# The hidden bias product moved from the prologue into the tile loop, and three chunks of the last two matrices' product split in a new order

## The chip, the cores and the metric

One Trainium2 chip, one of its cores. The metric is the device time in microseconds of one execution. TensorE multiplies into PSUM (8 banks of 128 x 512 float32), VectorE, ScalarE and GpSimd work element by element, and SyncE, ScalarE and GpSimd issue the loads and stores.

## The reference

Eight batches of 512 rows of 512 numbers (`x`) go through two layers, both added to `x`:

```python
# layer 1: windowed attention; h = layernorm(x), enc = ctx_1024 (8 x 512 x 512)
score = einsum('nqh,hk,nlk->nql', h, W_a, enc)      # only a window of +-16 rows around p_t counts
align = softmax(masked score) * gauss
x = x + tanh(concat([align @ enc, h]) @ W_c.T)

# layer 2: 64 slots, on xn = layernorm(x); S = slot_init for all batches
slot_mean = S.mean(axis=1)                          # the same row for all tokens
h = gelu(concat([xn, slot_mean]) @ w1 + b1)
alpha = softmax over the top 8 of (h @ w2 + b2) / (|tau| + 0.1)
si = (alpha^T xn) / sum(alpha)
gi = si @ Wih.T + bih;  gh = S @ Whh.T + bhh        # GRU gates; gh does not depend on x
S_new = (1 - z) * n + z * S
y = layernorm(S_new + self-attention(S_new)) * ln_g + ln_b
x = x + (alpha @ (y @ wvp + bvp)) @ wo + bo
```

What the change touches are constants: `Wp = wvp @ wo`, one 512 x 512 product made once; the constant part of the first layer of layer 2, `slot_mean @ w1[512:] + b1`, one bias per hidden unit (`hb`); and `gh = S @ Whh.T`.

## The kernel before, in words

The 4096 rows are 32 tiles of 128 rows (`NT`), four to a batch. A prologue prepares constants, a loop of 32 tile steps does layer 1 for tile s and, some steps later, the first part of layer 2 for the same tiles, and a tail runs the slots' update and the outputs. Each engine has its own hand-written instruction order; semaphores (`S("...")`) tie them together. An engine that waits holds everything behind it in its own order.

Float32 products are mostly done as split products (`mm3`, L455): each factor is a high part (rounded to fp32r) plus a low part (the rest), and three products hi*hi, lo*hi, hi*lo are added in PSUM (lines L456 to L458). A plain `pe.matmul` on F32 tiles is a full-precision product; the profile lists each of these as two instructions.

**Prologue.** On TensorE: warm-up products (L1550); `Wp` in banks 4 to 7 from `WvpT` and `Wo`, in four chunks k of 128 rows, chunks 0 and 1 in full precision (L1575), chunks 2 and 3 split (`SPLIT_WP`); ahead of chunk 3 the 12 transposes of the gathered windows (`turn_windows`, L1559), which wait for the indirect load `encw`; then 16 instructions of the hidden bias product `w1b` x `slotmean` into bank 3 (L1585); then the window product of WaT and the windows (L1617, 16 split blocks over four chunks k and four banks c), one row product (L1624), the window values (L1630), and the loop. Block c of chunk 0 of the window product waits for window part c, and c = 3 for `hb`, because bank 3 holds the bias until VectorE has added `b1` to it (L819).

On VectorE: window positions and masks (L754 to L791, among them four operations on 128 x 288, L775 to L778), the row sums of half of WaT (L782, after its load), the mean of the slots (L793, L794), a load of the flag into a register, the low parts of windows and of WaT (`windows`, `low_key_weights`), `hb`, the low parts of Wc1T (L841), and so on. On ScalarE: the Gaussian, the high parts for `SPLIT_WP` (L1252), the other sums of WaT, then, once all sums are there, WaT's high parts (L1262) and those of windows 1 and 2 (L1265). On GpSimd: the indirect loads (L579) and the low parts for `SPLIT_WP` (L637, L639), counted on `wcs`. On SyncE's queue: `win`, `WvpT`, `WaT`; a wait for the last chunks of `WvpT` and `Wo`; `w1b`; a wait for the gathered windows; `Wc2_raw`, `Wc1T`, four tiles of `xT` and `x`, `w1_raw`, `WhhT`.

**Tile step s** on TensorE (L1809): `score(s)` (12 instructions, waits for the low part of tile s and for the tanh of tile s - 2, which frees its bank), `turn_weights(s - 1)`, `right_half(s)`, at s = 1 `bias_row`, `context(s - 1)`, the first layer and logits of layer 2 where they are due, `extras(s)`, and `turn_rows(s - 2)`, which waits for ScalarE's normalised tile. `extras` holds the products `S @ Whh.T`: the r and z gates at step `GATES_STEP` = 1 into bank `SI` (L1641), the n gate one step later into `H1` (L1648), and two sets of transposes at steps 4 and 6. VectorE's step (L1028) goes: low part of tile s - 3, `scores_max(s)`, statistics of tile s + 3, `weights_of(s)` (the two operations on `stack`, L981 and L982, for which `turn_weights(s)` waits), `extras(s)`, `stats2(s - 1)`. Its `extras(0)` makes seven small constants, `extras(1)` splits `w1` (L929, L930), `extras(2)` adds a row (L933), steps 3 and 4 copy the gates out. GpSimd's step: `residual(s - 1)` (L604, waits for the tanh of that tile), `low_x(s + 2)` (L599), scales.

## Time and profile before

| | us |
|---|---|
| three runs | 348.90, 349.93, 349.70; median 349.7 |
| the profiled execution | 349.35, its span 347.4, mean granted clock of TensorE 0.993 |
| busy over the span | TensorE 329.5 (95%), VectorE 261.0 (75%), ScalarE 198.8 (57%), GpSimd 209.2 (60%) |
| chain that ended last | TensorE 56%, VectorE 14%, GpSimd 7%, ScalarE 7%, DMA 6% |

The span runs from the first to the last instruction; all times of rows are counted from its start. Two things are to be read here: which engine has no idle time in which stretch (busy time by stretch), and, where several engines hand over to each other, the timeline of each: when an operation starts, how long it lasts, and what is said in brackets of the idle time before it. An operation that lasts longer than others of its shape has been held inside.

### The profile page before, as it was taken

The page shows a single profiled execution, that of the slowest core. Times are in us where ns is not written, and L with a number is a line of the kernel's source. Part 1 is how long each engine was busy: PE and PEld are TensorE (multiplying, and loading weights), DVE is VectorE, ACT ScalarE, POOL GpSimd, SP SyncE. Part 2 cuts the span into 40 slices and gives each one's busy share as a digit, 9 for nine tenths or more (in the row PEclk, how much of TensorE's full clock was granted, in tenths as well). Part 3 has the DMA queues.
Part 4 walks back from the last instruction along what each step waited for, and adds up shares of the span by engine and source line. Part 5 has one row for each costly group of instructions (what it writes and reads, how often), then busy time and mean ns, then how long its engine had stood idle before and what let it go on. Part 6 is the DMA issues. An engine that isn't in the chain of part 4 may idle for free.

```text
span 347.4 us, 7118 instructions
## 1 busy us (share of the span) xinstructions
PE 329.5 (95%) x2320; PEld 284.3 (82%) x2320; DVE 261.0 (75%) x749; ACT 198.8 (57%) x406; POOL 209.2 (60%) x353
## 2 busy tenths in 40 slices
PE   8899998999998999999999999999999999999981
PEld 6597856999898998898989989986889886877750
DVE  5989898675789798788787877766953766477873
ACT  3367225567768759668569677666754336313521
POOL 5600156879687776974976884746575335235782
PEclk9999999999999999999999999999999999999997
DMA  7999975232323232232241200008900000000797
GB/s 271 261 321 353 343 216 182 93 114 69 109 74 114 71 98 88 62 119 65 62 122 62 86 9 2 0 0 271 314 1 2 1 2 0 0 0 3 291 393 283
DMA packets 40934, 42.79 MB, mean 123 GB/s; under 512 B 3245, under 2 KB 32045, under 8 KB 40898
## 3 DMA queue, kind: packets, MB, share of 16 engines
q1 hardware_dynamic: 38944, 40.19, 35.4%
q10 hardware_dynamic: 1666, 1.49, 1.3%
q0 software_dynamic: 288, 0.66, 0.7%
q8 instruction: 19, 0.31, 0.4%
q14 instruction: 17, 0.14, 0.1%
HBM read 32.18 MB, written 8.39 MB: 117 GB/s over the span
## 4 chain that ended last, share of the span: by engine, by line
PE 56%; DVE 14%; POOL 7%; issue 7%; ACT 7%; DMA 6%; SPq 1%; DVEq 0%; ACTq 0%; POOLq 0%
PE psum L456 13%; PE psum L457 12%; PE psum L458 12%; PE psum L1741 4%; PE psum L2003 3%; DMA xT<-in_xT 3%; POOL X L604 3%; PE psum L1770 3%; DMA encw<-in_enc,rowi 2%; ACT th L1320 2%; DVE st L971 2%; PE psum L1721 2%; PE psum L1805 1%; DVE xhT_lo L958 1%; PE psum L1952 1%
## 5 line engine op out<-in xcount | busy, mean ns | idle before, releaser
L456 PE MATMUL psum<-GW_hi,hT_hi 128*128 128x292 f32 (+1 forms) x256 | 78.6, 307 | 0.0
L458 PE MATMUL psum<-GW_lo,hT_hi 128*128 128x292 f32 (+1 forms) x256 | 74.0, 289 | 0.0
L457 PE MATMUL psum<-GW_hi,hT_lo 128*128 128x292 f32 (+1 forms) x256 | 73.9, 289 | 0.0
L604 POOL TENSOR_TENSOR X<-X,th 128x512 f32<-128x512 f32 x32 | 38.3, 1196 | 29.0 <-ACT th L1320 28.5
L456 PEld LDWEIGHTS psum<-GW_hi,hT_hi 128*128 128x128 f32 x256 | 48.5, 189 | 1.8 <-issue 1.4
L457 PEld LDWEIGHTS psum<-GW_hi,hT_lo 128*128 128x128 f32 x256 | 48.4, 189 | 0.0
L458 PEld LDWEIGHTS psum<-GW_lo,hT_hi 128*128 128x128 f32 x256 | 48.1, 188 | 0.0
L599 POOL TENSOR_TENSOR hT_lo<-xT,hT_hi 128x512 fp32r<-128x512 f32 x30 | 39.1, 1304 | 2.0 <-DVE stack L982 2.0
L971 DVE BATCH_NORM_STATS2 st<-X 128x6 f32<-128x512 f32 x32 | 22.2, 693 | 22.6 <-POOL X L604 22.6
L456 PE MATMUL psum<-xhT_hi,w_hi 128*128 128x256 f32 x128 | 38.0, 297 | 1.1 <-issue 1.0
L457 PE MATMUL psum<-xhT_hi,w_lo 128*128 128x256 f32 x128 | 36.1, 282 | 0.0
L458 PE MATMUL psum<-xhT_lo,w_hi 128*128 128x256 f32 x128 | 36.1, 282 | 0.0
L1301 ACT ACTIVATE e<-scm,nmr,rr 128x36 f32<-128x36 f32 x32 | 13.3, 417 | 28.8 <-DVE nmr L967 28.7
L456 PEld LDWEIGHTS psum<-xhT_hi,w_hi 128*128 128x128 f32 x128 | 24.3, 190 | 3.9 <-issue 3.8
L1307 ACT CAST aTs<-psum 108x128 fp32r<-108x128 f32 x32 | 8.6, 268 | 30.9 <-PE psum L1795 30.9
L1315 ACT ACTIVATE xh<-X,nm,r2all 128x512 f32<-128x512 f32 x31 | 25.0, 806 | 1.9 <-POOL nm L613 1.9
L457 PEld LDWEIGHTS psum<-xhT_hi,w_lo 128*128 128x128 f32 x128 | 24.4, 190 | 0.0
L458 PEld LDWEIGHTS psum<-xhT_lo,w_hi 128*128 128x128 f32 x128 | 24.3, 190 | 0.0
L456 PE MATMUL psum<-siT_hi,W_hi 128*128 128x256 f32 (+1 forms) x72 | 23.5, 326 | 0.0
L457 PE MATMUL psum<-siT_hi,W_lo 128*128 128x256 f32 (+1 forms) x72 | 23.1, 321 | 0.0
L458 PE MATMUL psum<-siT_lo,W_hi 128*128 128x256 f32 (+1 forms) x72 | 22.9, 318 | 0.0
L958 DVE TENSOR_TENSOR xhT_lo<-psum,xhT_hi 128x512 fp32r<-128x512 f32 x32 | 21.3, 666 | 1.5 <-ACT xhT_hi L1296 1.5
(316 smaller groups left out, 919.0 us busy)
## 6 DMA issues: line engine op xcount, KB each, us to landing
xT<-in_xT SPq DMA_DIRECT2D x32, 256.0 KB, 2.8
X<-in_x SPq DMA_DIRECT2D x32, 256.0 KB, 3.5
out<-ost SPq DMA_DIRECT2D x32, 256.0 KB, 2.8
WhhT<-in_WhhT SPq DMA_DIRECT2D x1, 3072.0 KB, 12.9
WihT<-in_WihT SPq DMA_DIRECT2D x4, 768.0 KB, 6.8
Wo<-in_wo ACTq DMA_DIRECT2D x4, 256.0 KB, 4.4
WvpT<-in_WvpT SPq DMA_DIRECT2D x4, 256.0 KB, 5.2
WaT<-in_WaT SPq DMA_DIRECT2D x1, 1024.0 KB, 12.1
```

The lines of the kernel that those rows point to most:

```text
L456: pe.matmul(out, w_hi, m_hi, start=start, stop=False)
L457: pe.matmul(out, w_lo, m_hi, start=False, stop=False)
L458: return pe.matmul(out, w_hi, m_lo, start=False, stop=stop)
L599: pool.tensor_tensor(hT_lo[:, t % 2, :, :], xT[:, t % 4, :, :], hT_hi[:, t % 2, :, :].bitcast(F32), ALU.subtract).then_inc(S("hl"), 1)
L604: pool.tensor_tensor(tile_x(r), tile_x(r), halves(th[:, :]), ALU.add).then_inc(S("x2"), 1)
L958: v.tensor_tensor(xhT_lo[:, :, dst], bank.rearrange("p (c n) -> p c n", c=KC), xhT_hi[:, :, dst].bitcast(F32), ALU.subtract).then_inc(S("x ...
L971: link(v.bn_stats(st2[:, :], tile_x(r)), "stat")
L1301: act.activation(e[:, :], scm[:, :], ACT.Exp, bias=nmr[:, :], scale=rr1[:, s % 4:s % 4 + 1], accum_out=esum[:, :]).then_inc(S("ex"), 1)
L1315: act.activation(halves((th if r == NT - 1 else xh)[:, :]), tile_x(r), ACT.Identity, bias=nm2[:, :], scale=r2all[:, r:r + 1]).then_inc(S(" ...
L1741: last = pe.matmul(SI[h * NS:(h + 1) * NS, 0:XW], al, X[:, TPB * b + q, h, :], start=q == 0, stop=q == TPB - 1)
L1770: last = pe.transpose(bank[:, c * P:(c + 1) * P], rows_of[:, c * P:(c + 1) * P], ident[:, :])
L2003: last = pe.matmul(out_banks(m)[par], w[at_b, :], mv[g][at_b, :], start=n == 0, stop=n == 2)
```

## The change

- **Hidden bias.** Its 16 products leave the prologue and come, as `hidden_bias`, into tile step 1 (`HIDDEN_STEP`), after `bias_row` and ahead of `context(0)`, into bank `SI` instead of bank 3. The mean of the slots on VectorE moves from the prologue to the end of its `extras(0)`, `hb` to the start of its `extras(2)`. The window product no longer waits for `hb`; ScalarE's gelu waits for it.
- **Gates.** `GATES_STEP` goes from 1 to 2, so the WhhT products and all that follows them (transposes, copies) come one tile step later, and the first of them waits for `hb`, which frees `SI`.
- **Wp.** Chunks 1, 2 and 3 are split instead of 2 and 3. Within a chunk the order is hi*hi for all four banks, then lo*hi, then hi*lo, each waiting for its own low part; the window transposes stand after chunk 3's hi*hi. The low parts are made by VectorE (`low_of_Wp`), two operations a chunk, among its mask operations and ahead of the WaT sums, instead of by GpSimd.
- **VectorE's order.** The WaT sums come last before the flag is loaded; before, they stood after the mask operations L775 to L778.
- **Loads.** SyncE waits for WaT alone, then loads `Wc2_raw`, `Wc1T`, the tiles, `w1_raw`, `w1b`, `WhhT`: `w1b` moves from ahead of `Wc2_raw` to behind `w1_raw`, and the wait for the gathered windows goes.
- Semaphore counts and the places in SBUF follow.

```diff
@@ -34,16 +34,16 @@
-HB_DONE, G_DONE, WM_DONE, EW_DONE = 1, 1, KC + 2, KC + 2
-
-
-HI_WA, HI_ENC, HI_WC1, HI_G, HI_GW, HI_EW = 4, 4 + KC, 6 + KC, 6 + 2 * KC, 6 + 3 * KC, 6 + 4 * KC
-BVZ_DONE, LOW_WP = 5, 5
-
-
-SUMS_DONE, MEAN_DONE, CHUNKS_DONE, LOW_WC1 = 2, 3, 4, 4
-
-SPLIT_WP = (2, 3)
+G_DONE, WM_DONE, EW_DONE, HB_DONE = 0, KC + 1, KC + 1, KC + 2 + NG
+
+
+HI_WA, HI_ENC, HI_WC1, HI_G, HI_GW, HI_EW = 6, 6 + KC, 8 + KC, 8 + 2 * KC, 8 + 3 * KC, 8 + 4 * KC
+BVZ_DONE, LOW_WP = 1, 1
+
+
+SUMS_DONE, CHUNKS_DONE, LOW_WC1, MEAN_DONE = 2, 3, 3, 4 + KC
+
+SPLIT_WP = (1, 2, 3)
 ENC_BANKS = 3
@@ -59,7 +59,7 @@
 SLOT_STEP = [TPB * b + 12 for b in range(NB)]
-BIAS_STEP, GATES_STEP = 1, 1
+BIAS_STEP, HIDDEN_STEP, GATES_STEP = 1, 1, 2
 WARM = 9
...
@@ -488,15 +491,14 @@
         sp.dma_start(WaT[:, :, :], chunks("WaT")).then_inc(S("in_wa"), 16)
-        sp.wait_ge(S(f"in_wo{KC - 1}"), 32)
-        sp.dma_start(w1b[:, :, :], chunks("w1", KC)).then_inc(S("in_w1b"), 16)
-        sp.wait_ge(S("encw"), 16 * NG)
+        sp.wait_ge(S("in_wa"), 16)
         sp.dma_start(Wc2_raw[:, :, :], chunks("WcT", KC)).then_inc(S("in_wc2"), 16)
         sp.dma_start(Wc1T[:, :, :], chunks("WcT")).then_inc(S("in_wc1"), 16)
         for t in range(4):
             xT_load(t)
             x_load(t)
         sp.dma_start(w1_raw[:, :, :], chunks("w1")).then_inc(S("in_w1"), 16)
+        sp.dma_start(w1b[:, :, :], chunks("w1", KC)).then_inc(S("in_w1b"), 16)
         sp.dma_start(WhhT[:, :, :], chunks("WhhT")).then_inc(S("in_whh"), 16)
         sp.wait_ge(S("flag"), 1)
@@ -632,11 +634,6 @@
             if s % 2 == 0 and live(s + 2):
                 scales1(s + 2)
-        for n, k in enumerate(SPLIT_WP):
-            pool.wait_ge(S("wa"), 2 * n + 1)
-            pool.tensor_tensor(Wvp_lo[:, n, :], WvpT[:, k, :], Wvp_hi[:, n, :].bitcast(F32), ALU.subtract).then_inc(S("wcs"), 1)
-            pool.wait_ge(S("wa"), 2 * n + 2)
-            pool.tensor_tensor(Wo_lo[:, n, :], Wo[:, k, :], Wo_hi[:, n, :].bitcast(F32), ALU.subtract).then_inc(S("wcs"), 1)
         pool.wait_ge(S("in_misc"), 16 * 4)
         pool.tensor_copy(bvz[:, :, 0:1], bvp.unsqueeze(2)).then_inc(S("wcs"), 1)
         pool.wait_ge(S("g_lo"), KC)
@@ -771,15 +768,23 @@
         link(v.tensor_copy(rsf[:, :], rsi[:, :]), "win")
         link(v.scalar_tensor_tensor(rend[:, :], pall, REACH, lenf[:, :], ALU.add, ALU.min), "win")
         link(v.tensor_scalar(rend[:, :], rend[:, :], float(T - 1), None, ALU.min), "win")
+
+        def low_of_Wp(k):
+            n = SPLIT_WP.index(k)
+            Wvp_hi, Wvp_lo, Wo_hi, Wo_lo = of_Wp[k]
+            v.wait_ge(S("wa"), 2 * n + 1)
+            v.tensor_tensor(Wvp_lo[:, :], WvpT[:, k, :], Wvp_hi[:, :].bitcast(F32), ALU.subtract).then_inc(S("wplo"), 1)
+            v.wait_ge(S("wa"), 2 * n + 2)
+            v.tensor_tensor(Wo_lo[:, :], Wo[:, k, :], Wo_hi[:, :].bitcast(F32), ALU.subtract).then_inc(S("wplo"), 1)
+
+        low_of_Wp(1)
         r3 = lambda a: a.rearrange("p (b j) -> p b j", b=NB)
         link(v.tensor_tensor(r3(ridx[:, :]), bc(rsf[:, :], WS, 2), bc(jrow[:, :], NB, 1), ALU.add), "win")
         link(v.tensor_tensor(r3(vlo[:, :]), r3(ridx[:, :]), bc(rast[:, :], WS, 2), ALU.is_ge), "win")
         link(v.tensor_tensor(r3(madd[:, :]), r3(ridx[:, :]), bc(rend[:, :], WS, 2), ALU.is_le), "win")
         link(v.tensor_tensor(vlo[:, :], vlo[:, :], madd[:, :], ALU.mult), "win")
-        v.wait_ge(S("in_wa"), 16)
-        for c in range(2, KC):
-            v.tensor_reduce(wsum[:, c:c + 1], WaT[:, c, :], AX.X, ALU.add).then_inc(S("v_prep"), 1)
+        low_of_Wp(2)
         link(v.tensor_reduce(anyv[:, :], r3(vlo[:, :])[:, :, 0:WIN], AX.X, ALU.max), "win")
         link(v.tensor_scalar(madd[:, :], vlo[:, :], 1.0, MASKED, ALU.subtract, ALU.mult), "win")
         link(v.memset(r3(madd[:, :])[:, :, UNI:WS], -MASKED), "win")
@@ -789,9 +794,10 @@
         v.tensor_scalar(flag[:, :], flagf[:, :], -1.0, float(NB), ALU.mult, ALU.add).then_inc(S("flag"), 1)
         v.wait_ge(S("gauss"), 2)
         v.tensor_scalar(gw[0:WP, :], gw[0:WP, :], geo[:, 1:2], None, ALU.max).then_inc(S("first_row"), 1)
-        v.wait_ge(S("in_misc"), 16 * 4)
-        link(v.tensor_reduce(slotmean[:, :], slotT[:, :, :], AX.X, ALU.add), "rt")
-        v.tensor_scalar(slotmean[:, :], slotmean[:, :], 1.0 / NS, None, ALU.mult).then_inc(S("v_prep"), 1)
+        low_of_Wp(3)
+        v.wait_ge(S("in_wa"), 16)
+        for c in range(2, KC):
+            v.tensor_reduce(wsum[:, c:c + 1], WaT[:, c, :], AX.X, ALU.add).then_inc(S("v_prep"), 1)
         v.wait_ge(S("flag"), 1)
         f = v.value_load(flag[0:1, 0:1], min_val=0, max_val=NB)
@@ -815,8 +821,6 @@
         for j in range(1, ENC_BANKS):
             windows(j)
         low_key_weights(1)
-        v.wait_ge(S("pre"), HB_DONE)
-        v.tensor_tensor(hb[:, :], banks[3][:, 0:HC], b1, ALU.add).then_inc(S("first_row"), 1)
         for k in range(2, KC):
             low_key_weights(k)
         with v.If(f > 0):
@@ -917,6 +921,7 @@
         def extras(s):
             if s == 0:
+                v.wait_ge(S("in_misc"), 16 * 4)
                 link(v.scalar_tensor_tensor(itau[:, :], tau, -1.0, tau, ALU.mult, ALU.max), "rt")
                 link(v.tensor_scalar(itau[:, :], itau[:, :], 0.1, None, ALU.add), "rt")
                 link(v.reciprocal(itau[:, :], itau[:, :]), "rt")
@@ -924,6 +929,12 @@
                 link(v.tensor_scalar(b2s[:, :], b2, itau[:, :], None, ALU.mult), "rt")
                 link(v.tensor_tensor(brz[:, 0:2 * KC], bih[:, 0:2 * KC], bhh[:, 0:2 * KC], ALU.add), "rt")
                 link(v.tensor_copy(brz[:, 2 * KC:], bhh[:, 2 * KC:]), "rt")
+            if s == HIDDEN_STEP - 1:
+                link(v.tensor_reduce(slotmean[:, :], slotT[:, :, :], AX.X, ALU.add), "rt")
+                v.tensor_scalar(slotmean[:, :], slotmean[:, :], 1.0 / NS, None, ALU.mult).then_inc(S("v_prep"), 1)
+            if s == HIDDEN_STEP + 1:
+                v.wait_ge(S("pre"), HB_DONE)
+                v.tensor_tensor(hb[:, :], SI[:, 0:HC], b1, ALU.add).then_inc(S("first_row"), 1)
             if s == 1:
                 v.wait_ge(S("in_w1"), 16)
                 link(v.tensor_copy(w1_hi[:, :, :], w1_raw[:, :, :]), "w1s")
@@ -1247,10 +1258,11 @@
         link(act.activation(gall[:, :], gall[:, :], ACT.Exp, scale=-1.0 / DEV))
         act.mul(gall[:, :], gall[:, :], 1.0 / T).then_inc(S("gauss"), 1)
-        for n, k in enumerate(SPLIT_WP):
+        for k in SPLIT_WP:
             act.wait_ge(S(f"in_wo{k}"), 32)
-            act.copy(Wvp_hi[:, n, :], WvpT[:, k, :]).then_inc(S("wa"), 1)
-            act.copy(Wo_hi[:, n, :], Wo[:, k, :]).then_inc(S("wa"), 1)
+            Wvp_hi, Wvp_lo, Wo_hi, Wo_lo = of_Wp[k]
+            act.copy(Wvp_hi[:, :], WvpT[:, k, :]).then_inc(S("wa"), 1)
+            act.copy(Wo_hi[:, :], Wo[:, k, :]).then_inc(S("wa"), 1)
         act.wait_ge(S("in_wa"), 16)
@@ -1321,6 +1333,7 @@
         def gelu(b, h):
             act.wait_ge(S("w1"), 4 * b + 2 * h + 2)
+            act.wait_ge(S("first_row"), 2)
             wait(act, S("lg"), 2 * b - 1)
             for o in range(HC):
                 act.activation(h1T[:, o, h * HT:(h + 1) * HT], HB[h][:, o * HT:(o + 1) * HT], ACT.Gelu,
@@ -1561,30 +1574,22 @@
                     last.then_inc(S("encT"), 1)
-        for k in range(KC):
-            pe.wait_ge(S(f"in_wo{k}"), 32)
-            if k in SPLIT_WP:
-                n = SPLIT_WP.index(k)
-                pe.wait_ge(S("wcs"), 2 * n + 2)
-            for c in range(KC):
-                at_c = slice(c * P, (c + 1) * P)
-                if k in SPLIT_WP:
-                    last = mm3(pe, banks[4 + c], Wvp_hi[:, n, at_c], Wvp_lo[:, n, at_c], Wo_hi[:, n, :], Wo_lo[:, n, :],
-                               False, k == KC - 1)
-                else:
-                    last = pe.matmul(banks[4 + c], WvpT[:, k, at_c], Wo[:, k, :], start=k == 0, stop=False)
-                if k == KC - 1:
-                    last.then_inc(S("wp_mm"), 1)
-            if k == KC - 2:
-                turn_windows()
-
-        pe.wait_ge(S("in_w1b"), 16)
-        pe.wait_ge(S("v_prep"), MEAN_DONE)
-        for o in range(HC):
-            for k in range(KC):
-                last = pe.matmul(banks[3][:, o:o + 1], w1b[:, k, o * P:(o + 1) * P], slotmean[:, k:k + 1],
-                                 start=k == 0, stop=k == KC - 1)
-        last.then_inc(S("pre"), 1)
+        for c in range(KC):
+            pe.wait_ge(S("in_wo0"), 32)
+            pe.matmul(banks[4 + c], WvpT[:, 0, c * P:(c + 1) * P], Wo[:, 0, :], start=True, stop=False)
+        for k in SPLIT_WP:
+            n = SPLIT_WP.index(k)
+            Wvp_hi, Wvp_lo, Wo_hi, Wo_lo = of_Wp[k]
+            for part, (w, m) in enumerate(((Wvp_hi, Wo_hi), (Wvp_lo, Wo_hi), (Wvp_hi, Wo_lo))):
+
+                pe.wait_ge(S("wa"), 2 * n + 2)
+                wait(pe, S("wplo"), 2 * n + part if part else 0)
+                for c in range(KC):
+                    last = pe.matmul(banks[4 + c], w[:, c * P:(c + 1) * P], m[:, :], start=False, stop=k == KC - 1 and part == 2)
+                    if k == KC - 1 and part == 2:
+                        last.then_inc(S("wp_mm"), 1)
+                if k == KC - 1 and part == 0:
+                    turn_windows()
         pe.wait_ge(S("gauss"), 2)
         pe.wait_ge(S("flag"), 1)
@@ -1611,8 +1616,6 @@
                     if c < ENC_BANKS:
                         pe.wait_ge(S("encWT"), max(LOW_WA[0], ENC_DONE[c]))
-                    else:
-                        pe.wait_ge(S("first_row"), 2)
                 at_c = slice(c * P, (c + 1) * P)
                 last = mm3(pe, banks[c][:, 0:NB * WS], WaT_hi[:, k, at_c], WaT_lo[:, k, at_c],
                            encWT_hi[:, k, 0:NB * WS], encWT_lo[:, k, 0:NB * WS], k == 0, k == KC - 1)
@@ -1636,6 +1639,7 @@
             if s == GATES_STEP:
                 pe.wait_ge(S("in_whh"), 16)
+                pe.wait_ge(S("first_row"), 2)
                 for k in range(KC):
                     for h in range(2):
                         last = pe.matmul(SI[h * NS:(h + 1) * NS, :], slotT[:, k, :], WhhT[:, k, h * D:(h + 1) * D],
@@ -1659,6 +1663,16 @@
                 for c in range(KC // 2):
                     last = pe.transpose(SI[:, c * P:(c + 1) * P], ghs[:, KC + c, :], ident[:, :])
                 last.then_inc(S("own"), 1)
+
+        def hidden_bias():
+
+            pe.wait_ge(S("in_w1b"), 16)
+            pe.wait_ge(S("v_prep"), MEAN_DONE)
+            for o in range(HC):
+                for k in range(KC):
+                    last = pe.matmul(SI[:, o:o + 1], w1b[:, k, o * P:(o + 1) * P], slotmean[:, k:k + 1],
+                                     start=k == 0, stop=k == KC - 1)
+            last.then_inc(S("pre"), 1)
         def bias_row():
@@ -1815,6 +1829,8 @@
                 right_half(s)
             if s == BIAS_STEP:
                 bias_row()
+            if s == HIDDEN_STEP:
+                hidden_bias()
             if live(s) and s:
                 context(s - 1)
             if s in TOPK_STEP:
```

## Rows read from the trace of the kernel before

**Rows 1.** Windows view, tile loop: stretch, its length, busy us (x instructions) of each engine.
```profile
61.40:245.00 183.60, 180.04 (x1445) 167.37 (x1446) 143.07 (x499) 129.15 (x271) 133.36 (x262) 1.00 0.27 82
```

**Rows 2.** Timeline, TensorE, prologue: start us, us, engine, line, operation, tiles, count.
```profile
4.93 7.13 PE L1575 MATMUL psum<-Wo,WvpT 128*128 128x512 f32 x16
...
17.31 0.48 PE L456 MATMUL psum<-Wo_hi,Wvp_hi 128*128 128x512 f32 x1
...
20.15 1.84 PE L1585 MATMUL psum<-slotmean,w1b 128*128 128x1 f32 x16
21.85 0.38 PE L456 MATMUL psum<-encWT_hi,WaT_hi 128*128 128x288 f32 x1
...
37.56 0.30 PE L456 MATMUL psum<-GW_hi,hT_hi 128*128 128x292 f32 x1
```

**Rows 3.** Timeline, VectorE, prologue; brackets: idle before it and who released it.
```profile
8.11 0.46 DVE L776 TENSOR_TENSOR vlo<-ridx,rast 128x288 f32<-128x288 f32 x1
8.60 5.68 DVE L777 TENSOR_TENSOR madd<-ridx,rend 128x288 f32<-128x288 f32 x1
...
15.25 1.28 DVE L782 TENSOR_REDUCE wsum<-WaT 128x1 f32<-128x512 f32 x2 [0.47 <-DMA WaT<-in_WaT]
...
18.00 0.41 DVE L793 TENSOR_REDUCE slotmean<-slotT 128x4 f32<-128x256 f32 x1
...
19.36 0.61 DVE L802 CAST encWT_hi<-psum 128x432 fp32r<-128x432 f32 x1 [0.75 <-issue]
...
21.19 1.11 DVE L805 TENSOR_TENSOR encWT_lo<-psum,encWT_hi 128x432 fp32r<-128x432 f32 x2
...
26.33 2.49 DVE L841 TENSOR_TENSOR Wc1T_lo<-Wc1T,Wc1T_hi 128x512 fp32r<-128x512 f32 x4
```

**Rows 4.** Timeline, ScalarE, prologue.
```profile
7.87 0.62 ACT L1252 CAST Wvp_hi<-WvpT 128x512 fp32r<-128x512 f32 x1 [0.88 <-DMA WvpT<-in_WvpT]
...
16.91 2.56 ACT L1262 ACTIVATE WaT_hi<-WaT,wneg 128x512 fp32r<-128x512 f32 x4
19.38 0.91 ACT L1265 CAST encWT_hi<-psum 128x432 fp32r<-128x432 f32 x2
```

**Rows 5.** Timeline, SyncE's DMA queue, first load after its second wait.
```profile
16.12 0.37 SPq L494 DMA_DIRECT2D Wc_raw<-in_WcT  x1
```

**Rows 6.** Timeline, TensorE, end of tile step 1 to score(4).
```profile
45.52 0.50 PE L1805 MATMUL psum<-EW,aTs 108*128 108x256 f32 x2
45.95 3.65 PE L1641 MATMUL psum<-WhhT,slotT 128*64 128x512 f32 x16
49.54 0.40 PE L456 MATMUL psum<-GW_hi,hT_hi 128*128 128x292 f32 x1
...
53.09 1.95 PE L1648 MATMUL psum<-WhhT,slotT 128*64 128x256 f32 x16
...
60.74 0.66 PE L1770 MATMUL psum<-ident,xh 128*128 128x128 f32 x4 [0.98 <-ACT xh L1315]
61.36 0.37 PE L456 MATMUL psum<-GW_hi,hT_hi 128*128 128x292 f32 x1
```

**Rows 7.** Timeline, VectorE, tile steps 0 to 2.
```profile
45.88 0.18 DVE L926 COPY brz<-vecs 128x4 f32<-128x4 f32 x1
...
47.91 1.29 DVE L981 TENSOR_SCALAR stack<-e,ev 128x72 fp32r<-128x72 f32 x1
49.23 1.19 DVE L982 SCALAR_TENSOR_TENSOR stack<-e,ev,stack 128x36 f32<-128x36 f32 x1
...
51.06 1.23 DVE L930 TENSOR_TENSOR w_lo<-w_raw,w_hi 128x1024 fp32r<-128x1024 f32 x1
...
55.40 0.68 DVE L933 TENSOR_TENSOR rows<-psum,rows 128x512 f32<-128x512 f32 x1
```

**Rows 8.** Timeline, GpSimd, tile step 1.
```profile
47.95 1.19 POOL L604 TENSOR_TENSOR X<-X,th 128x512 f32<-128x512 f32 x1 [1.92 <-ACT th L1320]
49.10 1.27 POOL L599 TENSOR_TENSOR hT_lo<-xT,hT_hi 128x512 fp32r<-128x512 f32 x1
```

5 lines of the change are left out of this document (4 added, 1 removed).

## The prediction

> **What bounds the kernel now.** I read the busy time by stretch first. From 61.4 to 245 us TensorE is busy 180.0 of 183.6 us [rows 1]: in the tile loop there is nothing left for it to wait for, so a step that starts late there ends late by the same amount, and work given to TensorE is paid in full unless it falls into a hole. The question is therefore by how much score(4), the product that opens tile step 4 at 61.36 [rows 6], comes earlier or later; from there on the same products stand in the same order but for two sets of transposes that move by one step each (steps 4 and 6 lose what steps 5 and 7 gain), a sum of zero. The timeline of TensorE in the prologue [rows 2] shows an unbroken line from 17.31 to 37.56. The other engines' timelines there [rows 3, 4] show why it can't start the window product much earlier: VectorE first has to sum WaT, turn the windows and make low parts, and ScalarE's rounding hangs on these sums. In steps 1 and 2 [rows 6] the 3.59 us of WhhT products (45.95 to 49.54) stand exactly where VectorE is busy with something that TensorE will need [rows 7]: they are cover, not only work.
>
> I keep the clock of the kernel before (the "old clock") and first shift all by what the prologue wins.
>
> **Part 1, the prologue up to the window product.** Removed from TensorE: the bias product, 1.70 us (20.15 to 21.85 [rows 2]), and the full-precision product of chunk 1. A full-precision chunk costs 3.56 us (7.13 for two), a split one 2.84 (17.31 to 20.15), so 0.7 less. TensorE would be ready some 2.5 us or more ahead of 21.85. But it then waits. VectorE's new line: it is free for the first low part at about 7.6 (one mask operation, 0.49, ahead of the row at 8.11 [rows 3]), when ScalarE, idle for 0.88 us ahead of 7.87 [rows 4], can have made the first high part. Six low parts at 0.62 (2.49 for four of that shape [rows 3]) are 3.7; four mask operations at 0.49 are 2.0, the 5.68 us of L777 being a stretched one; the small operations between the sums and 18.00 are 1.5. That is 14.8. The two sums take 1.28 and give 16.1 if WaT has landed by 14.8, and 16.5 if it lands as before at 15.2. So the sums end where they ended before (16.5), and ScalarE's four WaT roundings (2.47) and two window roundings (0.91 [rows 4]) start 0 to 0.4 us earlier and end at about 19.9 to 20.3. VectorE's 0.75 of loading the flag and 1.83 for window part 0 and WaT part 0 (19.36 to 21.19 [rows 3]) are done by 18.7 to 19.1, but windows 1 and 2 (0.55 each) wait for ScalarE, and the third of 16 blocks of the product starts at 20.5 to 20.9, as if the first had at 19.7 to 20.1. Gain: 21.85 less that, 1.75 to 2.15; I take **1.9**. VectorE's later line (three adds, the low parts of Wc1T) runs without a hole and moves by the same, and the loads come earlier, because SyncE now waits for WaT instead of the gathered windows (16.12 [rows 5]) and w1b is no longer among the first. Bounds: 0.9, if VectorE comes 1 us later to the sums than reckoned (GpSimd is still writing the gather's descriptors when the first low parts run, and no row shows the two together); 2.6 to 2.8, with 2.6 taken, if the two window waits cost nothing (21.85 less 19.1). The low parts that leave GpSimd cost nothing there; nothing of it is waited for until the tile loop.
>
> **Part 2, the tile loop's first steps, old clock.** VectorE gets the mean of the slots after the last operation of its step 0 (ends 46.06 [rows 7]), two operations that took 0.61 (18.00 to the 0.75 us ahead of 19.36 [rows 3]): ready at 46.7. TensorE gets there at 45.52 [rows 6], waits 1.2 us, loads weights (0.2), runs 1.70 and starts context(0) at 48.6; the tanh of tile 0, which must free a PSUM bank for score(2), follows its end: 48.6 + 0.5 + 0.7 (an estimate from the context's 0.50 and a 0.6 to 0.8 us ScalarE pass) is 49.85. score(2) started at 49.54 before; now 49.85, with the WhhT products still to do. w1b is covered: it stands ahead of WhhT in the queue, and WhhT was there at 45.95 without a wait.
>
> Score, turning, right half and context of step 2 take 3.55 (49.54 to 53.09), so TensorE is at the moved WhhT product at 53.4. There it now waits for hb, an addition of 0.15 us on VectorE, because the bank in which the hidden bias lies is the one these products write. Behind that wait stand, on TensorE, the WhhT products, the turning of tile 0 and score(3); nobody else is held by it. When is hb there? Before, VectorE reached that place (its step 2 extras) at 55.40 [rows 7]. The mean adds 0.62. The two operations on the stack, 1.29 and 1.19 us long, had been stretched by GpSimd's residual and low part at 47.95 to 50.4 [rows 8]; GpSimd now starts these at 49.9, so the stack is done 2.0 us sooner relative to its start and the same 2.4 us of GpSimd fall on the 1.23 us w1_lo operation instead. If w1_lo ends with GpSimd, as the stack operations did, at 52.4, then tile 0's statistics start there instead of at 52.3, 0.1 late; hb comes before the operation that stood at 55.40, and with its own 0.15 is at 55.65. Ends: 54.3, if neither engine holds the other (statistics at 51.1, when the residual is there); 56.8, if w1_lo only starts once GpSimd is through. I take **55.65**, since both stack operations ended within 0.1 us of GpSimd's: TensorE waits 2.2 us. The products take 3.59 (59.25), turning tile 0 0.66 (59.9). Step 3: 3.55 (63.45), the n products 1.95 (65.4), turning tile 1 0.66 (66.1), and score(4) at 66.1 against 61.36, **+4.7**. Filled in that are two holes: 0.98 us ahead of the row at 60.74, and about 0.5 in step 2 (60.74 - 0.98 - 3.55 - 0.66 is 55.55, the start of turning tile 0, and the n products ended at 55.04).
>
> The sum is 4.7 - 1.9 = **+2.8 us**. The profiled execution took 349.35 (span 347.4), which gives 352.15; the median of the runs, 0.35 above it, gives **352.5**. Bounds: 4.7 - 1.3 (hb at 54.3) - 2.6 = +0.8, 350.5; 4.7 + 1.15 - 0.9 = +4.95, 354.65.
>
> A rule weighed against the trace: VectorE's L777 starts at 8.60 and L981 at 47.91, the latter 0.04 us ahead of GpSimd's 1.19 us operation at 47.95 and yet it lasts 1.29 us [rows 3, 7, 8]; the one that began first lost. The Trainium skill (SBUF — State Buffer, "Who interferes with whom") says that an operation of VectorE with two SBUF inputs and one of GpSimd contend for a port pair and that "Whoever issues first gets the shared pair for the whole instruction". By that rule w1_lo, started 0.2 us before the residual, would keep the ports until 50.9, the statistics would start at 52.1, hb would be there at 55.3 and the result would be 352.2; by the row it is 352.5. The rule also speaks for this change, since GpSimd's four low parts no longer stretch L777; the trace shows that VectorE after that sat waiting for WaT, so that the 5.2 us were mostly free.
>
> **The rivals.**
> Rival 1, VectorE is there in time (faster). If the mean and hb were ready before TensorE asks, what is left is -1.9 in the prologue, +1.7 for the bias product in the loop, and the two holes filled, 1.4 together: -1.6, 348.1. For it: the mean needs only slotT, and could be made while TensorE works. Against: on VectorE it stands behind everything else of step 0, whose last row, 45.88, comes after TensorE's at 45.52 already. It decides from where the two waits and the tanh together cost less than 1.6 us.
> Rival 2, only the first wait binds: with the mean late (+1.4 with the weight load) and the tanh (+0.8) but hb in time: 348.1 + 2.2 = 350.3, within what can't be told from no change. It wants VectorE at hb by 53.4, 0.9 us ahead of my own lowest bound.
> Rival 3, the prologue doesn't win what it should: chunk 1's split and the new place of the low parts put 3.7 us on VectorE ahead of the WaT sums, which were the late thing already. If WaT's landing plus these make the sums end at 18 instead of 16.5, the window product starts 0.4 us earlier only: +4.3, 354.0. For it: the sums now stand last in VectorE's list. Against: 14.8 against 15.2 above, a margin of 0.4 us.
>
> **How the numbers follow.** The forecast gets 0.60, rival 3 0.13, rival 2 0.15, rival 1 0.12. The predicted time is the forecast's, 352.5. Rival 1 is left out of the range, and the low end lies at 350.0, which takes in rival 2; the high end at 354.8, for the upper bound 354.65 and rival 3. A measurement of this kernel can tell about 0.3% (1.05 us) from no change: faster means under 348.65, slower over 350.75. Rival 1 is faster (0.12); rival 2 and the bottom of the forecast are the same (0.15 + 0.03 = 0.18); the rest, 0.70, is slower.
>
> **What would show each step right or wrong** in the profile of the changed kernel: the WaT sums ending at 16.1 to 16.6; the third block of the window product at 20.5 to 20.9; score(0) at 35.7 instead of 37.56; a hole of TensorE of about 1.3 us ahead of the bias product, put down to the mean's scaling on VectorE; none or under 0.3 us ahead of score(2); a hole of about 2 us ahead of the WhhT products, put down to hb; no hole ahead of the turning of tiles 0 and 1; score(4) at 66.1 - 1.9 = 64.2. The prediction is wrong if the hole ahead of the WhhT products is missing or under 1 us, or if score(0) has moved by less than 1 or more than 2.6 us, or if the steps after 4 don't keep the shift that score(4) has: then the loop had slack that its busy time hides.

## The result

| | before | changed |
|---|---|---|
| seven runs each, median | 349.34 us | 350.81 us (350.69 to 352.15) |
| ratio | | 1.006, 95% interval 1.0043 to 1.0077 |
| profiled execution: span, mean granted clock | 347.4 us, 0.993 | 348.7 us, 0.983 |

The change makes the kernel slower by 0.6% by the ratio, by 0.4% between the two medians. 350.81 us is inside the predicted range and on the predicted side, but half the predicted distance, 1.5 instead of 2.8 us between the medians, and not by the steps as I put them.

Three of all runs (370.33, 373.57 and 409.59 us, granted clock 0.75 to 0.85) fell in a second, slower state and are left out of the ratios and of the counts below.

**By stretch.** Windows view (stretch, its length, busy us and instructions of each engine, granted clock, DMA share, GB/s), first one row of the kernel before, then two of the changed kernel:

```profile
37.50:61.40 23.90, 21.96 (x155) 16.44 (x154) 20.63 (x61) 8.99 (x22) 12.23 (x25) 1.00 0.75 229
```

```profile
37.50:61.40 23.90, 20.72 (x130) 16.65 (x129) 16.23 (x55) 7.25 (x18) 12.14 (x24) 0.86 0.75 215
61.40:245.00 183.60, 181.02 (x1462) 167.91 (x1461) 142.88 (x494) 130.54 (x273) 134.10 (x263) 1.00 0.27 79
```

The new thing is the 0.86: in the stretch of steps 0 to 3 the granted clock of TensorE, 1.00 in the kernel before, is below full speed. And the last row has 1.0 us more busy time than its counterpart [rows 1]: in the tile loop there were waits to be lost.

**Prologue.** TensorE, VectorE, ScalarE and SyncE's queue, the rows that answer to [rows 2 to 5]:

```profile
18.54 0.30 PE L459 MATMUL psum<-encWT_hi,WaT_hi 128*128 128x288 f32 x1
...
20.21 0.41 PE L459 MATMUL psum<-encWT_hi,WaT_hi 128*128 128x288 f32 x1 [1.12 <-DVE encWT_lo L811]
...
20.73 0.41 PE L459 MATMUL psum<-encWT_hi,WaT_hi 128*128 128x288 f32 x1
...
35.57 0.30 PE L459 MATMUL psum<-GW_hi,hT_hi 128*128 128x292 f32 x1
```

```profile
14.07 0.68 DVE L778 TENSOR_TENSOR Wo_lo<-Wo,Wo_hi 128x512 fp32r<-128x512 f32 x1
14.73 1.28 DVE L800 TENSOR_REDUCE wsum<-WaT 128x1 f32<-128x512 f32 x2
...
19.55 1.12 DVE L811 TENSOR_TENSOR encWT_lo<-psum,encWT_hi 128x432 fp32r<-128x432 f32 x2 [1.51 <-ACT encWT_hi L1277]
```

```profile
16.48 2.56 ACT L1274 ACTIVATE WaT_hi<-WaT,wneg 128x512 fp32r<-128x512 f32 x4
18.95 0.91 ACT L1277 CAST encWT_hi<-psum 128x432 fp32r<-128x432 f32 x2
```

```profile
14.72 0.37 SPq L495 DMA_DIRECT2D Wc_raw<-in_WcT  x1
```

VectorE is done with its six low parts at 14.7, when WaT is there. TensorE can start the window product at 18.54, 3.3 us before the row at 21.85 [rows 2], but stands 1.12 us for the low parts of windows 1, which wait for ScalarE's rounding of the windows, behind its four roundings of WaT. The third block starts at 20.73, score(0) at 35.57: 1.99 us gained between these two executions. Three more kernels with the same prologue had score(0) at 35.34, 35.34 and 35.84, and `turns_late`, whose prologue is that of the kernel before, at 36.88, so that other pairs give 1.0 to 2.2 us.

**Steps 0 to 3.** TensorE, the rows that answer to [rows 6]:

```profile
41.23 0.32 PE L1809 MATMUL psum<-ident,stack 128*108 128x128 f32 x1 [0.88 <-DVE stack L993]
...
45.24 2.15 PE L1673 MATMUL psum<-slotmean,w1b 128*128 128x1 f32 x16 [1.27 <-DVE slotmean L934]
47.25 0.77 PE L1819 MATMUL psum<-EW,aTs 108*128 108x256 f32 x2
48.89 0.58 PE L459 MATMUL psum<-GW_hi,hT_hi 128*128 128x292 f32 x1 [0.87 <-ACT th L1332]
...
49.75 0.45 PE L459 MATMUL psum<-GW_hi,hT_hi 128*128 128x292 f32 x1
...
50.48 0.45 PE L459 MATMUL psum<-GW_hi,hT_hi 128*128 128x292 f32 x1
...
54.22 0.40 PE L1819 MATMUL psum<-EW,aTs 108*128 108x256 f32 x2
54.77 3.65 PE L1645 MATMUL psum<-WhhT,slotT 128*64 128x512 f32 x16 [0.16 <-DVE hb L937]
...
64.58 0.38 PE L459 MATMUL psum<-GW_hi,hT_hi 128*128 128x292 f32 x1
```

The three holes of 0.88, 1.27 and 0.87 us come first. Then look at the distance of the rows at 48.89, 49.75 and 50.48: three products apart, they are 0.73 us from each other where the same triple takes 0.40 us in the kernel before. The granted clock is at its lower level, 1.2 GHz, from 46.8 to 53.5 us:

```profile
46.70:53.50 6.80, 5.93 (x27) 5.63 (x27) 4.50 (x12) 2.07 (x6) 4.05 (x7) 0.50 0.79 214
```

It falls within the last part of the bias product. From score(2) to context(1) it takes 5.33 us; before, it took 3.22 (the 3.55 from 49.54 to 53.09 [rows 6], less the context). The hole ahead of the WhhT products, forecast at 2 us, is 0.16.

VectorE and GpSimd in the same stretch, answering to [rows 7, 8]:

```profile
44.92 0.17 DVE L934 TENSOR_SCALAR slotmean<-slotmean 128x4 f32<-128x4 f32 x1
...
46.81 0.26 DVE L992 TENSOR_SCALAR stack<-e,ev 128x72 fp32r<-128x72 f32 x1
...
47.99 1.22 DVE L941 TENSOR_TENSOR w_lo<-w_raw,w_hi 128x1024 fp32r<-128x1024 f32 x1
50.37 0.69 DVE L982 BATCH_NORM_STATS2 st<-X 128x6 f32<-128x512 f32 x1 [1.15 <-POOL X L606]
...
52.19 0.20 DVE L975 TENSOR_TENSOR scm<-psum,madd 128x36 f32<-128x36 f32 x1 [0.90 <-PE psum L461]
...
54.47 0.15 DVE L937 TENSOR_TENSOR hb<-psum,vecs 128x2 f32<-128x2 f32 x1
```

```profile
48.82 1.45 POOL L606 TENSOR_TENSOR X<-X,th 128x512 f32<-128x512 f32 x1 [4.41 <-ACT th L1332]
```

VectorE itself waited 0.90 us at 52.19 for the slow score(2), and so had hb only at 54.47, when TensorE was about to ask for it. Without this wait hb would have started at 53.57, no sooner, since the statistics at 50.37 wait for GpSimd's residual. So only about 1 us of the 2.1 us of slow products reaches the WhhT products: at full clock TensorE would have waited for hb for the rest.

**Behind step 4.** score(4) is 3.22 us late (64.58 against 61.36), score(9) 1.96, score(31), the last, 1.44, the span 1.3. So 1.8 of the 3.2 us came back.

### The profile page after: what moved, and what is told of

Read it like the earlier page. It is cut to its first block, busy times and chain, and to the rows that moved or that the text cites. A ratio compares the mean times of both kernels' runs of the same rounds, so it can differ in the third digit from the quotient of the medians.

```text
span 348.7 us, 7137 instructions
## 1 busy us (share of the span) xinstructions
PE 330.8 (95%) x2324; PEld 287.5 (82%) x2324; DVE 257.3 (74%) x755; ACT 200.3 (57%) x408; POOL 205.6 (59%) x349
## 4 chain that ended last, share of the span: by engine, by line
PE 64%; DVE 13%; DMA 6%; ACT 6%; issue 5%; POOL 3%; SPq 1%; DVEq 0%; ACTq 0%; POOLq 0%
PE psum L459 15%; PE psum L460 14%; PE psum L461 14%; PE psum L1755 4%; PE psum L2019 3%; DMA WaT<-in_WaT 3%; PE psum L1784 3%; DMA xT<-in_xT 3%; PE psum L1819 2%; PE psum L1735 2%; POOL X L606 1%; ACT th L1332 1%; DVE st L982 1%; DVE xhT_lo L969 1%; DVE st L746 1%
## 5 line engine op out<-in xcount | busy, mean ns | idle before, releaser
L459 PE MATMUL psum<-GW_hi,hT_hi 128*128 128x292 f32 (+1 forms) x256 | 79.6, 311 | 0.9 <-ACT th L1332 0.9
L460 PE MATMUL psum<-GW_hi,hT_lo 128*128 128x292 f32 (+1 forms) x256 | 74.7, 292 | 0.0
L459 PEld LDWEIGHTS psum<-GW_hi,hT_hi 128*128 128x128 f32 x256 | 49.3, 193 | 1.7 <-issue 1.5
L460 PEld LDWEIGHTS psum<-GW_hi,hT_lo 128*128 128x128 f32 x256 | 49.3, 192 | 0.0
L461 PEld LDWEIGHTS psum<-GW_lo,hT_hi 128*128 128x128 f32 x256 | 48.9, 191 | 0.0
L1308 ACT CAST xhT_hi<-psum 128x512 fp32r<-128x512 f32 x32 | 18.7, 585 | 10.4 <-PE psum L1784 10.3
```

Of the source, the lines that this page charges most:

```text
L459: pe.matmul(out, w_hi, m_hi, start=start, stop=False)
L460: pe.matmul(out, w_lo, m_hi, start=False, stop=False)
L461: return pe.matmul(out, w_hi, m_lo, start=False, stop=stop)
L1308: act.copy(xhT_hi[:, :, dst], bank.rearrange("p (c n) -> p c n", c=KC)).then_inc(S("xhh"), 1)
```

## The experiments

All twelve ran beside the kernel before; a ratio is against its runs in the same comparison (medians 348.8 to 349.6 us). A profiled execution can come out of its prologue up to 2.2 us earlier or later than another of the same code (36.88 to 39.05 us), so I compare distances: from the start of score(0) to that of score(4), and on to score(9) and to the last score. The last column is how long ScalarE waited in step 4 for VectorE's `nmr` (it is used below).

| kernel | score 0 to 4 | 4 to 9 | 9 to 31 | clock, 37.5 to 61.4 | ratio, interval | wait for nmr |
|---|---|---|---|---|---|---|
| before | 23.80 | 29.53 | 135.33 | 1.00 | | 1.81 |
| changed | 29.01 | 28.27 | 134.81 | 0.86 | 1.006, 1.0043 to 1.0077 | 0.33 |
| wp_only | 24.70 | 29.55 | 134.73 | 1.00 | 0.997, 0.9949 to 0.999 | 1.79 |
| loop_only | 29.16 | 28.27 | 135.30 | 0.86 | 1.0083, 1.0055 to 1.011 | 0.33 |
| mean_early | 27.05 | 28.27 | 135.08 | 0.86 | 1.0007, 0.9985 to 1.0029 | 0.33 |
| gates_back | 25.67 | 28.97 | 134.73 | 1.00 | 1.0029, 1.0009 to 1.0049 | 1.24 |
| gates_first | 24.48 | 29.01 | 134.80 | 1.00 | 0.9961, 0.9942 to 0.998 | 1.25 |
| filler | 28.08 | 28.27 | 134.76 | 0.93 | 1.0048, 1.0028 to 1.0068 | 0.33 |
| filler_all | 28.27 | 28.27 | 134.96 | 0.93 | 1.0016, 0.9995 to 1.0037 | 0.33 |
| gates_only | 23.45 | 28.66 | 135.37 | 1.00 | 1.0009, 0.9989 to 1.0029 | 0.96 |
| holes | 24.93 | 29.53 | 134.75 | 1.00 | 0.9951, 0.9931 to 0.9972 | 1.79 |
| best | 23.34 | 29.51 | 134.92 | 1.00 | 0.9934, 0.9908 to 0.996 | 1.79 |
| turns_late | 23.76 | 29.53 | 135.41 | 1.00 | 1.0004, 0.9983 to 1.0025 | 1.78 |
| best_turns | 24.02 | 29.52 | 134.98 | 1.00 | 0.9932, 0.9908 to 0.9955 | 1.79 |

**1. Each half of the change alone.** `loop_only`: the kernel before with only the second part.

```diff
 # TensorE, prologue: the 16 products w1b x slotmean into banks[3] and their waits removed
-BIAS_STEP, GATES_STEP = 1, 1
+BIAS_STEP, HIDDEN_STEP, GATES_STEP = 1, 1, 2
 # mean at the end of extras(0), hb at the start of extras(2), hidden_bias in step 1
```

> The kernel before with the loop part of the change alone: hidden bias product in tile step 1, gates a step later, mean and hb in VectorE's loop; the product Wp, its low parts and the loads stay as before. Cover theory (the loss is TensorE waiting in steps 1 and 2 for VectorE's mean and hb, with the WhhT products no longer standing in VectorE's late places): without the mean's 0.61 us VectorE is done for the window product 0.6 to 1.0 us sooner than TensorE began it, so score(0) at 36.6 to 37.0 instead of 37.56; from there to score(4) as in the changed kernel, 29.0 us instead of 23.8, score(4) at 65.6 to 66.0; the end 1.0 to 1.2 us later than the changed kernel's, about 352. Rival (the product Wp's new split brings nothing): the same time as the changed kernel, 350.9, with score(0) at 35.6.

`wp_only`: the kernel before with only the first (three chunks split, low parts on VectorE, WaT sums last); the bias product and the order of the loads stay where they were. So the new load order is in neither half, and its own share is not measured.

```diff
-SPLIT_WP = (2, 3)
+SPLIT_WP = (1, 2, 3)
 # low_of_Wp(1), (2), (3) on VectorE, sums of WaT behind them; the mean after the sums
```

> The kernel before with the Wp part alone: three chunks split in the new order, low parts by VectorE, WaT sums last; hidden bias, gates and loads as before (the mean made right after the WaT sums). Cover theory: the loop is as before, 23.8 us from score(0) to score(4), and the prologue's own gain is what TensorE's line allows: transposes at 16.2 as before (the gathered windows land then), Wp done at 19.2, bias product until 20.9, window product from there, 0.9 us earlier than 21.85: score(0) at 36.6, total 348.5. Rival (the low parts on VectorE cost as much as they save): score(0) at 37.4 or later, total 349.4 or more.

Measured: `loop_only` 352.05 us, score(0) at 36.28 (0.3 sooner than expected), with the clock and the holes of the changed kernel ahead of the bias product and of score(2); `wp_only` 348.66 us, score(0) at 36.93. The parts add up within their intervals, 1.0083 and 0.997 to 1.0053 against 1.006. The prologue's work wins 0.3%, the loop's part costs 0.8%. That part gains 1.3 us in the prologue, which the bias product leaves, and costs 5.4 in steps 0 to 3 (29.16 against 23.80). Of the 0.6 us that `wp_only` wins up to score(0), steps 0 to 3 take 0.9 back (24.70; TensorE waits 1.55 us for the stack), which was not expected. Its gain of 0.3% stands in its median alone: the profiled execution took 349.62 us, 1 us over that median, and its span, 347.5, is no shorter than that of the kernel before. I can't trace the gain.

**2. The mean early.** The two operations of the mean go on VectorE behind the low parts of windows 0 and WaT 0, where it waits for ScalarE (19.55 above, 1.51 us); all else is the changed kernel.

```diff
+        v.wait_ge(S("in_misc"), 16 * 4)
+        link(v.tensor_reduce(slotmean[:, :], slotT[:, :, :], AX.X, ALU.add), "rt")
+        v.tensor_scalar(slotmean[:, :], slotmean[:, :], 1.0 / NS, None, ALU.mult).then_inc(S("v_prep"), 1)
@@ extras
-            if s == HIDDEN_STEP - 1: ...
```

> The changed kernel with one edit: the mean of the slots is made in the prologue, in VectorE's idle 1.5 us ahead of window part 1, instead of at the end of its step 0. Cover theory: the 1.27 us hole ahead of the bias product goes, score(2) starts 1.2 us sooner, and hb follows the same chain (residual of tile 0, its statistics, scores of tile 2), 1.3 to 2.3 us sooner, so the WhhT products start at 52.5 to 53.5 instead of 54.8 and the total is 348.7 to 349.7. Clock theory (the holes matter because the granted clock fell to its lower level, matmuls 0.244 us apart instead of 0.133, from 48.9 to 53.4, after two holes of 1.27 and 0.87 us): with one hole left of two the fall may stay away, which takes another 0.9 us off the WhhT products' start at most, since VectorE's chain is next; if it falls as before the gain is 1.3 us. Rival (hb's chain does not hang on the mean): WhhT products at 54.8 as before, total 350.9.

Measured: 349.97 us, 0.3 above the range expected, WhhT products at 52.81 and no wait for hb, score(0) at 35.60, so 1.96 us less in steps 0 to 3; yet TensorE stood 0.87 us ahead of score(2) for the tanh and ran it at the lower clock all the same. With the WhhT products in step 2, the late mean cost 2 us of 5.2.

**3. The gates back in step 1.** `gates_back` is the changed kernel with its late mean; `gates_first` has the early mean too. In both the bias lies in two spare columns of H1, so that SI is free for the WhhT products.

```diff
-BIAS_STEP, HIDDEN_STEP, GATES_STEP = 1, 1, 2
+BIAS_STEP, HIDDEN_STEP, GATES_STEP = 1, 1, 1
-                pe.wait_ge(S("first_row"), 2)     # ahead of the WhhT products
...
+            pe.wait_ge(S("ew"), 2)                # in hidden_bias
-                    last = pe.matmul(SI[:, o:o + 1], ...
+                    last = pe.matmul(H1[:, HALF + o:HALF + o + 1], ...
...
-            if s == HIDDEN_STEP + 1:     # hb
+            if s == HIDDEN_STEP + 2:     # and hb is read from H1
```

> The changed kernel with the WhhT products back in step 1 (GATES_STEP 1); the mean stays at the end of VectorE's step 0, the bias product lies in two spare columns of H1, so that it doesn't stand in the way of SI, and hb is added in VectorE's step 3. Theory A (the place of the gates carries the loss: without 3.65 us of cover in front of score(2), TensorE waits for the tanh and then runs score(2) to context(1) at the lower clock): the hole of about 1.3 us ahead of the bias product stays, there is none ahead of score(2), the clock of 37.5 to 61.4 us is 0.97 or more, score(2) starts at 51.9 to 52.6, score(4) at 61.0 to 61.7, time 348.6 to 349.8, that is within 0.2% of the kernel before and 1 to 2 us under the changed kernel. Theory B (the mean's late place carries the loss): score(4) at 63.5 or later and 350.3 or more, since the wait of 1.27 us is still there.

> The same with the WhhT products back in tile steps 1 and 2 and the bias product in another bank (the second hidden bank, columns 256 and 257), so that nothing waits for hb but gelu. Cover theory: prologue gain 2.0 as in the changed kernel, the bias product costs its 1.7 us in step 1, the holes of the kernel before ahead of turning tiles 0 and 1 (0.5 and 0.98 us) take back 0.5 to 1.4 of it, no hole in step 1: score(4) at 59.7 to 60.6, total 347.7 to 348.7, no fall of the granted clock. Clock theory alone: the changed kernel less what the fall cost, 2.1 us at most, 348.8 or more. Rival (prologue gain is given back later by slack in the loop): 349.4, as before.

TensorE in `gates_back`:

```profile
45.41 1.92 PE L1673 MATMUL psum<-slotmean,w1b 128*128 128x1 f32 x16 [1.22 <-issue]
...
51.18 0.40 PE L459 MATMUL psum<-GW_hi,hT_hi 128*128 128x292 f32 x1
...
51.69 0.30 PE L459 MATMUL psum<-GW_hi,hT_hi 128*128 128x292 f32 x1
...
52.09 0.30 PE L459 MATMUL psum<-GW_hi,hT_hi 128*128 128x292 f32 x1
```

The hole of 1.2 us ahead of the bias product is the changed kernel's, but score(2) follows 3.65 us of WhhT products without a hole, and its triples are 0.4 to 0.5 us apart. 3.34 of the 5.2 us are gone in the profile (29.01 to 25.67). The profiled execution took 348.88 us, inside what I expected (348.6 to 349.8), but it is the fastest of its twelve; their median, 349.84, is just above (section 4 has what sets it apart). `gates_first`: 348.28 us, score(4) at 59.97, faster than both kernels. The two places together carry the loss. In the profiled distances the WhhT products' place is the larger part (3.34 or 2.57 us, taken back first or second, against 1.19 or 1.96 for the mean). In the ratios it is not: 0.3% or 0.5% for the products, 0.7% or 0.5% for the mean, with intervals of 0.2% to either side. Which is the larger is not shown.

**4. What lets the clock fall?** Products of ones, whose result nobody reads, are put into TensorE's holes.

```diff
+        def filler(n):
+            for _ in range(n):
+                pe.matmul(SI[:, P:2 * P], ones[:, :], ones[:, :], start=True, stop=True)
@@ step 1, ahead of hidden_bias(): filler(3); step 2, ahead of score(2): filler(2)
```

> The changed kernel with work added and nothing taken out: five products of a 128 x 128 matrix of ones into columns of the bank SI that nobody reads, three of them behind right_half in step 1 (ahead of the bias product, where TensorE stands 1.27 us waiting for the mean) and two ahead of score(2) (where it waits 0.87 us for the tanh). Theory A: the granted clock fell at score(2) because of what TensorE did just before, two waits and 16 one-column products in 4 us; with columns streaming into these holes it stays at 2.4 GHz: matmuls of score(2) 0.13 us apart instead of 0.244, the row of 37.5 to 61.4 us near 1.00 instead of 0.86, score(2) to context(1) 3.2 to 3.5 us instead of 5.33; TensorE then reaches the WhhT products about 1.9 us sooner and finds hb not there: a hole of 0.3 to 1.2 us, and score(4) at 63.3 to 64.0 instead of 64.58. Time 349.7 to 350.5. Theory B: the fall has another cause (the place in the program, or something that lasts too long to be bridged by five products): the clock row stays at 0.86 and score(4) at 64.6 to 64.9, time 350.8 to 351.2. If only one part holds, the clock falls later and by less.

In `filler_all` two stand ahead of turn_weights(0), four ahead of hidden_bias, three ahead of score(2).

> The changed kernel with nine products of ones instead of five: two ahead of turning tile 0's weights (hole 0.55 with none there), four behind right_half ahead of the bias product (hole 0.40 left with three), three ahead of score(2) (hole 0.42 left with two). With five, the clock still fell at score(2), but for 3.0 us instead of 4.5. Theory A (idle time of TensorE is what lets it fall): the holes are 0 to 0.3 each, and the clock stays at 2.4 GHz or falls for under 1.5 us: clock row 0.96 or more, context(1) at 50.7 to 51.5 instead of 52.34 when score(0) is at 35.3; then the hole for hb is 1.5 to 2.3 us instead of 0.86, so that the WhhT products start at 53.4 to 53.7 all the same, score(4) at 63.2 to 63.6 and the time stays at 350.3 to 350.8. Theory B (the 16 one-column products are enough by themselves, busy though they are): clock row 0.93 or less, holes filled all the same.

And `gates_only`, the kernel before with the gates late and nothing else, holes without bias product:

```diff
-BIAS_STEP, GATES_STEP = 1, 1
+BIAS_STEP, GATES_STEP = 1, 2
```

> The kernel before with GATES_STEP 2 alone: the WhhT products leave step 1, nothing else is added there; bias product, mean and all else stay in the prologue. TensorE then has holes ahead of turning tile 0's weights (about 1.3) and ahead of score(2) (0.9, tanh), but neither the mean's wait of 1.3 nor the 16 one-column products. Theory A (the clock falls because of the mean's wait and the one-column products together with the holes): granted clock of 37.5 to 61.4 us at 0.97 or more, score(2) at 46.7 to 47.1, WhhT products 3.3 to 3.6 later without a wait, score(4) at 60.4 to 61.2; with 1.5 us given back later, time 1.5 to 2.3 us under the kernel before. Theory B (the holes alone let it fall): clock row 0.86 to 0.93, score(2) to context(1) 4.5 to 5.3 instead of 3.2, score(4) at 61.8 to 63.0, and a time within 1 us of the kernel before.

`filler_all`, its windows row and TensorE:

```profile
37.50:61.40 23.90, 22.57 (x154) 18.39 (x154) 16.96 (x57) 8.34 (x20) 13.51 (x25) 0.93 0.79 222
```

```profile
45.02 1.92 PE L1673 MATMUL psum<-slotmean,w1b 128*128 128x1 f32 x16 [0.18 <-DVE slotmean L934]
...
48.15 0.38 PE L459 MATMUL psum<-GW_hi,hT_hi 128*128 128x292 f32 x1 [0.20 <-ACT th L1332]
...
48.78 0.45 PE L459 MATMUL psum<-GW_hi,hT_hi 128*128 128x292 f32 x1
...
49.51 0.45 PE L459 MATMUL psum<-GW_hi,hT_hi 128*128 128x292 f32 x1
...
53.79 3.65 PE L1645 MATMUL psum<-WhhT,slotT 128*64 128x512 f32 x16 [0.49 <-DVE hb L937]
```

`gates_only`, the same:

```profile
37.50:61.40 23.90, 21.72 (x153) 16.79 (x153) 20.42 (x60) 8.90 (x21) 11.97 (x24) 1.00 0.72 210
```

```profile
48.33 0.37 PE L456 MATMUL psum<-GW_hi,hT_hi 128*128 128x292 f32 x1 [1.55 <-ACT th L1320]
...
48.82 0.30 PE L456 MATMUL psum<-GW_hi,hT_hi 128*128 128x292 f32 x1
...
49.21 0.30 PE L456 MATMUL psum<-GW_hi,hT_hi 128*128 128x292 f32 x1
...
50.80 0.32 PE L1795 MATMUL psum<-ident,stack 128*108 128x128 f32 x1 [0.62 <-DVE stack L982]
```

In `filler_all` no hole of step 1 is above 0.46 us, and the triples of score(2) are still at 0.73 us after the second; in `gates_only` there is a hole of 1.55 and one of 0.62, and they are at 0.40. Filling the holes didn't keep the clock up, it shortened the fall: the clock was at its lower level for 6.8 us in the changed kernel, in `loop_only` and in `mean_early`, for 3.4 us in `filler` (47.3 to 50.8) and `filler_all` (48.4 to 51.9). And in this execution of `gates_only` the holes without the bias product brought no fall in the loop. Times: 350.61 us for `filler`, between the two ranges expected, 349.83 for `filler_all`, 0.5 lower than expected. What all falls in the profiled executions have in common are the 16 one-column products, at whose end or up to 2 us behind which they begin. The strongest row for that is one I had not looked for. In the profiled execution of `gates_only`, whose prologue is the old one, the clock fell behind the bias product in its old place:

```profile
19.65 1.84 PE L1585 MATMUL psum<-slotmean,w1b 128*128 128x1 f32 x16
...
25.11 0.44 PE L456 MATMUL psum<-encWT_hi,WaT_hi 128*128 128x288 f32 x1
...
25.83 0.44 PE L456 MATMUL psum<-encWT_hi,WaT_hi 128*128 128x288 f32 x1
...
27.04 0.29 PE L456 MATMUL psum<-encWT_hi,WaT_hi 128*128 128x288 f32 x1
...
27.44 0.30 PE L456 MATMUL psum<-encWT_hi,WaT_hi 128*128 128x288 f32 x1
```

The 16 blocks of the window product are 0.40 us apart at full clock (27.04 to 27.44); while the clock is low, from 23.3 to 26.7, they are 0.72 (25.11 to 25.83). In the kernel before and `turns_late`, the same code, and in `wp_only`, the same 16 products ahead of the same window product, there is no fall. So it comes in some executions and not in others. The Trainium skill (TensorE: Matmul & The Clock Gate, the part on the clock gate) says that the clock follows how busy the array has lately been, and that the count runs free of the kernel, so that one kernel can see a different number of slow products at its start from run to run. The two prologues agree with that, some 20 us further on: the same code with slow products and without. The fall also goes with the late score(0) of `gates_only`, 39.05.

**What the other runs say of the clock.** One profiled execution is little for a thing that comes and goes, but every run has its mean granted clock on record. In all fourteen profiled executions the clock is low at the very end of the span, where TensorE has nothing to do; with no other fall, as in eight of them, the mean is 0.992 to 0.996. The six with a fall have 0.983 to 0.992. So a mean of 0.991 or less points to a fall ahead of that end, though not to its place, and 0.992 can still hide a short one (`filler_all`):

| bias product | gates | runs with a mean clock of 0.991 or less |
|---|---|---|
| in the prologue | step 1 | before (three comparisons) 17 of 94, wp_only 1 of 12, turns_late 3 of 12 |
| in the prologue | step 2 | gates_only 8 of 11 |
| whole, in step 1 | step 2 | changed 5 of 7, loop_only 8 of 8, mean_early 10 of 12, filler 6 of 12, filler_all 5 of 11 |
| whole, in step 1 | step 1 | gates_back 11 of 12, gates_first 8 of 12 |
| two halves, steps 1 and 2 | step 1 | holes 0 of 12, best 1 of 6, best_turns 1 of 12 |

Three readings follow. First, the profiled executions of `gates_back` and `gates_first` have the highest clock of their twelve (0.994 and 0.996): their row of 1.00 is not the rule, and it is not shown that the WhhT products keep the clock up. What goes with a high clock is the product in two halves. Second, `gates_only` moves no one-column product, and yet its clock is lower in most runs, so idle time as a cause (theory A of `filler_all`) is not refuted; the two causes are not parted here. Third, in the changed kernel the fall does not set the time: its two runs with 0.992, which leave room for a short fall at most, took 350.81 and 350.87 us, the five with less had a median of 350.81. That fits hb being waited for wherever the clock doesn't take the time. What decides a fall is open.

With five fillers the hole for hb was back, 0.86 us, and WhhT started at 53.60 instead of 54.77: where the clock doesn't take the time, hb does. `gates_only` gained in the profile what was expected (score(2) 9.28 us after score(0), score(4) 23.45, without a wait for hb, and 0.87 us less from 4 to 9), but its median is within 0.3% of the kernel before, not 1.5 to 2.3 us under. Its three runs with a mean clock of 0.995 or more took 347.89 to 348.75 us, its other eight, 349.66 by their median: falls of the clock go with a good part of that miss, not with all of it.

**5. Where do the 1.3 us behind step 4 come from?** The step from score(4) to score(9) takes 28.27 us in every kernel with late gates and the bias product in step 1, 29.5 in the kernel before. Either it is the new place of the transposes and copies, or slack. `turns_late` moves those alone.

```diff
@@ VectorE extras
-GATES_STEP + 2, + 3, + 4, + 6
+GATES_STEP + 3, + 4, + 5, + 7
@@ TensorE extras, the transposes
-GATES_STEP + 3, + 5
+GATES_STEP + 4, + 6
```

> The kernel before with one thing moved: the two sets of gate transposes on TensorE go from steps 4 and 6 to steps 5 and 7, and VectorE's copies and additions for them one step later too (steps 4, 5, 6, 8 instead of 3, 4, 5, 7); the WhhT products stay in step 1, the bias product in the prologue. From score(4) to score(13) the kernel before takes 53.56 us, and each of the four kernels so far with the gates one step later takes 51.98 to 52.0, whether its score(4) was 1.3, 2.1 or 3.2 us late. Theory A (the 1.5 us come back because of where transposes, copies and additions stand, whatever the lateness): score(4) as before within 0.2, score(4) to score(13) at 51.9 to 52.3, the hole of 0.57 us ahead of the context in step 8 gone, score(8) to score(9) 6.7 instead of 7.57; time 1.2 to 1.6 us under the kernel before. Theory B (slack that only a late TensorE uses up): 53.3 to 53.6, hole there, no difference in time.

> The fastest kernel so far (mean early, WhhT products in step 1, bias product in two halves in the holes, ScalarE's rounding of windows 1 and 2 ahead) with the transposes, copies and additions of the gates one step later as well. Theory A (they give time back by their place): score(4) at 57.9 to 58.3, score(4) to score(13) 51.9 to 52.3 instead of 53.16, time 345.0 to 345.5 where its predecessor had 346.25. Theory B (only a late TensorE wins it): 346.0 to 346.5.

Theory A falls twice: 29.53 and 29.52 us, ratios 1.0004 and 0.9932 (`best` 0.9934). The last column of the table says what goes with it. ScalarE, timeline, its exponential of step 4 in `turns_late`, `gates_first` and the changed kernel:

```profile
64.69 0.42 ACT L1301 ACTIVATE e<-scm,nmr,rr 128x36 f32<-128x36 f32 x1 [1.78 <-DVE nmr L967]
```

```profile
63.48 0.42 ACT L1313 ACTIVATE e<-scm,nmr,rr 128x36 f32<-128x36 f32 x1 [1.25 <-DVE nmr L978]
```

```profile
67.16 0.42 ACT L1313 ACTIVATE e<-scm,nmr,rr 128x36 f32<-128x36 f32 x1 [0.33 <-DVE nmr L978]
```

Wait 1.8, 29.5 us; 1.25, 29.0; 0.96, 28.7; 0.33, 28.3: fourteen kernels in four classes and one order. My reading, which no run here tries: in the kernel before, a ring of ScalarE (exponential, normalised tile, tanh), GpSimd (residual, which needs the tanh) and VectorE (statistics, then `nmr`) still runs late behind TensorE in step 4, and TensorE waits for it, some 0.35 us in step 4 and 0.57 at 87.26 in step 8 for a ScalarE copy that stands behind a gelu (the 0.98 us at 60.74 [rows 6] lie ahead of score(4) and don't count here). But it isn't simply that a TensorE which comes later finds the ring ready: `wp_only` and `holes` reach score(4) 0.9 and 1.1 us later after their score(0) than the kernel before and win nothing, `gates_only` reaches it 0.35 us sooner and wins 0.87. The wait for `nmr` goes with the gain; what sets it is open.

**6. Filling the holes.** `holes` is `gates_first` with the bias product in two halves, one ahead of turning tile 0's weights in step 1, one ahead of turning tile 0's rows in step 2.

```diff
@@ step
+            if s == HIDDEN_STEP:
+                hidden_bias(0)          # ahead of turn_weights(s - 1)
+            if s == HIDDEN_STEP + 1:
+                hidden_bias(1)          # behind extras(s)
```

> The kernel with the mean early and the WhhT products in step 1, and in addition the bias product cut into two halves of 0.85 us that stand where TensorE waits: half 0 ahead of the turning of tile 0's weights in step 1 (hole 0.88, for VectorE's stack), half 1 ahead of the turning of tile 0's rows in step 2 (hole about 0.3). Theory A (those holes are waits for other engines, which do not depend on TensorE): the hole of 0.88 is filled, context(0) at 44.8 to 45.0 instead of 45.65, score(4) at 59.1 to 59.4 instead of 59.97, time 347.3 to 347.9 where its predecessor had 348.28. Theory B (the product is not free in a hole: behind it the turning starts later because VectorE's operation is measured from TensorE's score(1), or the clock falls on the one-column products): score(4) at 59.9 or later, 348.2 or more.

`best` also changes ScalarE's order in the prologue.

```diff
         for c in range(KC):
             act.activation(WaT_hi[:, c, :], ...)
-        for j in range(1, ENC_BANKS): ...
+            if c == 0:
+                for j in range(1, ENC_BANKS): ...
         high_x(0)
-        high_x(1)
         for c in range(KC): ... G_hi
+        high_x(1)
```

> The kernel with the halves of the bias product in the holes, and in the prologue ScalarE rounds windows 1 and 2 right behind WaT's first part instead of behind all four parts (and makes G's high part ahead of the second tile's). The window product had a hole of 1.1 to 1.3 us ahead of its second block, for VectorE's low parts of windows 1, put down to ScalarE's order. Theory A (ScalarE's order is what is late): the hole is under 0.4, score(0) at 34.3 to 35.0 instead of 35.5, score(4) at 58.0 to 58.9, time 346.3 to 347.3. Theory B (behind it the loads or VectorE's own line are next: the low parts of WaT and windows take VectorE 4.8 us in whatever order, so the hole only moves to a later block): score(0) at 35.2 to 35.5 and 0 to 0.3 us gained.

`holes`: context(0) comes 9.08 us after score(0) instead of 10.16, but 0.87 us of it are waited again at the turning of tile 1 (0.27 before), and score(0) to score(4) is 24.93, not shorter. 347.13 us, ratio 0.9951 against 0.9961: no difference that these intervals show. The profiled execution, 348.84 us, is one of the slower of its twelve, with score(0) at 36.55, so that its distances don't stand for the others. In `best`, ScalarE and TensorE:

```profile
16.95 0.92 ACT L1278 CAST encWT_hi<-psum 128x432 fp32r<-128x432 f32 x2
```

```profile
19.33 0.40 PE L459 MATMUL psum<-encWT_hi,WaT_hi 128*128 128x288 f32 x1
...
34.71 0.30 PE L459 MATMUL psum<-GW_hi,hT_hi 128*128 128x292 f32 x1
```

The windows are rounded 2.0 us sooner than in the changed kernel, the hole of 1.1 to 1.3 us is gone and score(0) is at 34.71. 346.25 us, 0.66% under the kernel before and some 1.2% under the changed one. It has the lowest median, with `best_turns` (346.28), though its interval (six runs) overlaps that of `holes`.

## Why the prediction was right, and where not

- **Prologue, 1.9 us: right.** 1.99. The third block at 20.73 was forecast at 20.5 to 20.9; the sums ended at 16.0, against 16.1 to 16.6. That it fits to 0.1 us is luck, since other pairs of executions give 1.0 to 2.2. Rival 3 had no ground.
- **Wait for the mean, 1.2: right.** 1.27.
- **Tanh ahead of score(2), "none or under 0.3": wrong.** 0.87. The sign contradicted the sum it came from, which has the context done at 49.1 and score(2) at 49.85, a hole of 0.75; the sum was near. But score(2) was to start 12.29 us after score(0) and started after 13.32. Of the 1.03 us between, 0.33 lie ahead of the bias product: VectorE's line up to the mean moved by 1.63 us (44.25 against 45.88 [rows 7]) where TensorE's moved by 1.99. From the start of the bias product to that of context(0) it took 2.01 instead of 1.70, and from context(0) to score(2) 1.64 instead of 1.25, 0.27 of it the context itself at the lower clock. The remaining 0.1 is the hand-over to ScalarE's pass and back, for which the estimate had nothing.
- **Clock: not foreseen.** 2.1 us in score(2) to context(1), of which about 1 reached the WhhT products. The 0.993 of the kernel before gave no hint of it: its clock is 1.00 from 0 to 340 us and low only at the end of the span.
- **Wait for hb, 2.2: failed as it showed itself, its cause held.** 0.16 in the changed kernel; by the text's own words the prediction is wrong there. The slow clock took its place: hb came when it was to come (WhhT at 53.75 by the forecast, 53.60 in `filler`, 53.79 in `filler_all`, where less is lost to the clock), but TensorE no longer came early. Whoever comes second pays nothing; 2.1 and 2.04 us swapped places, and the sum hardly moved. That hb's time fits is luck all the same: the forecast had tile 0's statistics wait for a w1_lo held 1.3 us by GpSimd. They waited for the residual instead, which ended at 50.27, 1.1 us after the 49.2 that the forecast has for it (51.1 less 1.9), because the bias product, the context and so the tanh came late and the residual itself took 1.45 us instead of 1.19.
- **w1_lo held by GpSimd: wrong.** 1.22 us, unheld, and the stack operations 0.26 each. It started 0.83 us before the residual, which lasted 1.45 instead of 1.19. In `mean_early` the residual (46.47) was first, and both later operations waited for the one ahead, as the rows show:

```profile
46.95 2.09 DVE L941 TENSOR_TENSOR w_lo<-w_raw,w_hi 128x1024 fp32r<-128x1024 f32 x1
```

```profile
46.47 1.49 POOL L606 TENSOR_TENSOR X<-X,th 128x512 f32<-128x512 f32 x1 [2.58 <-ACT th L1332]
47.91 2.26 POOL L601 TENSOR_TENSOR hT_lo<-xT,hT_hi 128x512 fp32r<-128x512 f32 x1
```

  w_lo is held from 46.95 to 47.96, the end of the residual, and runs until 49.04; GpSimd's low part at 47.91 is held for that long and ends 1.13 us later. By the Trainium skill (SBUF — State Buffer, "Who interferes with whom") the first one issued gets the shared pair for its whole length, and these rows agree with it: 2.09 and 2.26 us instead of 1.22 and 1.28. My row for the contrary, 0.04 us between two starts, was too close a race to rest on.
- **score(4), 28.54 us after score(0): 29.01.** +1.03 up to score(2), -0.17 to score(3), -0.39 to score(4). Right in sum by two errors of opposite sign in step 2.
- **"A sum of zero" behind step 4: wrong.** -1.26 us to score(9). This is the step on which most of the distance from 352.5 to 350.8 hangs, and the prediction's own sign for it: the steps after 4 didn't keep the shift. TensorE's 180.0 of 183.6 us busy [rows 1] hid it: 3.6 us of idle time in that stretch are enough to take back 1.3. A further 0.5 us up to the last score is in `wp_only` too, whose loop there is the old one, and so can't be told from the spread of executions.

What it came to: 1.99 won, 5.21 lost in steps 0 to 3, 1.78 back, 1.44 in all.

## What to carry to other kernels

Before work is moved out of a stretch, ask what it covers: 3.65 us of products whose operands had long been there stood where the first tiles' tanh and statistics were due, and the work put there instead had to wait itself. When the busy time says that an engine has nothing left to wait for, add up its few idle us all the same: part of a delay can come back within some steps. Two delays that overlap are not added: with the clock up, hb was late; with the clock down, it was in time. And where an effect comes in some executions only, look at the numbers that every run leaves before you read a cause from one profile.

## What the hardware showed that I had not expected

- TensorE's granted clock fell from 2.4 to 1.2 GHz for 3.4 or 6.8 us, at the end of a run of 16 products of one column (1.8 us) or up to 2 us behind it (0.93 or 0.86 in the row of 23.9 us; triples of products 0.73 us apart instead of 0.40). Holes of 1.55 and 0.62 us without such products left it at 2.4 in one execution, but most runs of that kernel have a lower mean clock. In the prologue it fell in one profiled execution of the four that have the bias product there, for 3.4 us; its score(0) came 1.5 to 2.2 us later than in the two of the same code that kept the clock.
- The same products in two halves of eight, 13 to 14 us apart, go with a higher clock: a mean of 0.991 or less in 2 of 30 runs, against 19 of 24 with the product whole (`gates_back`, `gates_first`).
- VectorE and GpSimd hold each other for whole operations, and the hold passes on: 2.09 us on one, 2.26 on the other, from 0.48 us between their starts.
- The same prologue code started score(0) at 36.88, 37.56 and 39.05 us in three profiled executions, and that of `gates_first` and `holes` at 35.49 and 36.55. Absolute times across kernels would have misread both `holes` and `gates_only`.
